# Twelve of the sixteen steps of each pass of a two-layer attention kernel written as a hardware loop instead of straight code

## The chip, the cores and the metric

The kernel runs on one core of one Trainium2 chip. The core has five engines that each run their own instruction stream: PE (TensorE, matrix products), DVE (VectorE), ACT (ScalarE), POOL (GpSimd) and SP (SyncE, which here issues all DMAs). They meet only through semaphores. The metric is the device time of one execution in microseconds (us), as the median of several.

## The reference

Two transformer layers over x of shape (16, 256, 256), 16 heads of 16, with a context of the same shape. Cut to what is computed:

```
layer 0:  t = ln(x);  x += attn(t, t, mask) @ Wo + bo;  x += ctx @ Wg + bg
          x += relu(ln(x) @ W1 + b1) @ W2 + b2
layer 1:  t = ln(x);  x += attn(t, t, causal) @ Wo
          t = ln(x);  x += attn(t, ctx, no mask) @ Wo
          x += relu(ln(x) @ w1 + b1) @ w2 + b2
attn:     p = softmax(q k^T / 4 + bias) per head;  p @ v
```

## The kernel before

The work is cut into three passes over the batch: pass 0 is layer 0, pass 1 is the causal self-attention of layer 1, pass 2 its cross-attention and the perceptron behind it. A pass has 16 tasks, one for each batch element of 256 tokens, so there are 48 tasks. Weights are kept as a high and a low part, and the dense products are three matmuls each (line 451, and line 713 for the second matrix of the perceptron).

The program is a software pipeline. A `Step` s looks at six tasks at once: `nxt2` (s+2, input loaded and normalised), `nxt` (s+1, its q, k, v made and sent through DRAM into `q_stack` and `k_stack`), `cur` (s, scores and softmax, head by head), `prev` (s-1, output projection), `old` (s-2, perceptron) and `older` (s-3, whose store must be through). Each step has 16 slots, one per head of `cur`. In every slot each engine does its share for that head (PE: scores at line 509, transposes or keyed scores at 523 and 557, products with v at 587) and a fixed piece of the other tasks' work. The order on each engine is that of the code: there is no scheduler. `s_ps` and `t_ps` have two buffers each, so PE cannot run more than two heads ahead of DVE (`u_done`) and ACT (`e_done`, `pt_even`, `pt_odd`).

Every wait names a semaphore and a value that it must have reached. `Event.after` and `DmaEvent.after` work that value out from the task: with a batch number known when the program is built it is a constant. Both also have a form for a task whose batch is `2 * i + c`, with `i` the counter of a loop; this form is a sum of a constant and a multiple of `i`.

In the kernel before, `steps` calls the body of each engine for s = -2 to 49, one after the other. So each engine's program is 52 steps of straight code, without a branch inside them. Three things depend on the number s: the loading of weight units (`UNIT_LOAD_AT`) and their splitting (`UNIT_AT`), and the first task of a pass. They lie in the steps -2 to 1, 14 to 18 and 30 to 33.

Of the kernel before, what the change touches and what calls it, by code (L numbers as in the profile page):

```python
# [32 lines left out]
B, S, D = 16, 256, 256  # L33
H, HD = 16, 16
# [6 lines left out]
NPASS = 3  # L41
# [3 lines left out]
NTASK = NPASS * B  # L45
# [58 lines left out]
        self.prev, self.old, self.older = at(-1), at(-2), at(-3)  # L104

def steps(body):

    for s in range(-2, NTASK + 2):
        body(Step(s))  # L110

class Event:
# [31 lines left out]
def two_layers(nc, x, ctx, mask, wa, wm1, wm2, cols, rows, ident, out):  # L145
    with ExitStack() as es:
# [179 lines left out]
        def _(sp):  # L326
# [11 lines left out]
            def slot(st, h):  # L338
                if st.s is not None and (st.s, h) in UNIT_LOAD_AT:
                    u = UNIT_LOAD_AT[st.s, h]  # L340
                    if u:
                        sp.wait_ge(unit_hi, u)
                        sp.wait_ge(unit_lo, u)
                    dram, place, _, _ = unit_io(u)
                    sp.dma_start(place, dram).then_inc(unit_landed, 16)
# [43 lines left out]
                if h == 7 and has(st.nxt):  # L389
# [8 lines left out]
                    for m in range(KC):  # L398
                        heads = slice(8 * m, 8 * m + 8)
                        if st.prev:  # L400
                            done = s_mm if has(st.prev, (0,)) else st_mm
                            sp.wait_ge(done.sem, done.after(st.prev, 8 * m + 8))
                            sp.sem_inc(passed, 1)
                        sp.wait_ge(q_written[m].of(t), q_written[m].after(t))
                        sp.sem_inc(passed, 1)
                        row = 0
                        for part, n in RUNS:
                            sp.dma_start(q_stack[row:row + n * HD, t.par, heads].rearrange("r h s -> r (h s)"),
                                         parts[t.par, 0, m, part].rearrange("d h s -> d (h s)").unsqueeze(1)
                                         .to_broadcast([HD, n, H // KC * S])).then_inc(stacked[m].of(t), 16)  # L410
                            row += n * HD
                        sp.wait_ge(k_written[m].of(t), k_written[m].after(t))
                        sp.sem_inc(passed, 1)
                        row = 0
                        for _, n in RUNS:
                            sp.dma_start(k_stack[row:row + n * HD, t.par, heads].rearrange("r h s -> r (h s)"),
                                         parts[t.par, 1, m, 0:n].rearrange("j d h s -> d j (h s)"))\
                                .then_inc(stacked[m].of(t), 16)
                            row += n * HD
# [9 lines left out]
                if h == 15 and has(st.old, MLP):  # L429
# [2 lines left out]
                    dst = x_mid[0, st.old.b] if st.old.p == 0 else out[st.old.b]  # L432
                    sp.dma_start(tokens(dst), y_sb[:, :, :]).then_inc(stored.of(st.old), 16)

            steps(lambda st: [slot(st, h) for h in range(H)])
            for b in (B - 2, B - 1):
                sp.wait_ge(stored.of(Task(NPASS - 1, b)), stored.after(Task(NPASS - 1, b)))
                sp.sem_inc(passed, 1)
# [3 lines left out]
        def _(pe):  # L442
# [162 lines left out]
            def slot(st, h):  # L605
# [124 lines left out]
                if t:  # L730
                    values(st, t, c)

            steps(lambda st: [slot(st, h) for h in range(H)])

        @block.scalar
        def _(act):
# [43 lines left out]
            def slot(st, h):  # L781
# [95 lines left out]
                if has(st.cur, (0,)):  # L877
                    probs(st, h)

            steps(lambda st: [slot(st, h) for h in range(H)])  # L880

        @block.vector
        def _(dve):
# [69 lines left out]
            def slot(st, h):  # L954
# [146 lines left out]
                if st.s is not None:  # L1101
                    for u in UNIT_AT.get((st.s, h), ()):
                        dve.wait_ge(unit_landed, 16 * (u + 1))
                        unit_users_done(dve, u)
                        _, place, hi, _ = unit_io(u)
                        v.tensor_copy(hi, place).then_inc(unit_hi, 1)

            dve.sem_inc(y_done.sem, 1)
            steps(lambda st: [slot(st, h) for h in range(H)])  # L1110

        @block.gpsimd
        def _(pool):
# [43 lines left out]
            def slot(st, h):  # L1158
# [51 lines left out]
                if st.s is not None:  # L1210
                    for u in UNIT_AT.get((st.s, h), ()):
                        pool.wait_ge(unit_hi, u + 1)
                        _, place, hi, lo = unit_io(u)
                        sub(lo, place, hi, unit_lo)

            steps(lambda st: [slot(st, h) for h in range(H)])

# [31 lines left out]
```

## Time and profile before

| | |
|---|---|
| median of 3 runs | 1629.67 us (1625.86 to 1632.24) |
| profiled execution | 1625.86 us, its span 1624.1 us |
| granted TensorE clock, mean of the span | 0.97 |
| PE busy | 1448.7 us (89%) |
| DVE, ACT, POOL busy | 1193.5, 1033.5, 835.1 us |
| DMA | 187.07 MB |

The profile is a hardware record of one execution. "PE" is the matmuls, "PEld" the loading of the stationary operand, which overlaps them. Waits, semaphore instructions, register instructions and branches are not counted as busy. Where an engine stood idle and nothing that the profile knows released it, the profile says "issue". The chain is the series of instructions and waits that ended last, followed back from the end.

### The profile page before, as it was taken

What the parts mean: (1) busy time and instruction counts of PE and PEld (TensorE: products, weight loads), DVE (VectorE), ACT (ScalarE), POOL (GpSimd) and SP (SyncE); (2) the same over time, 40 slices, a digit from 0 to 9 for tenths busy, and PEclk for the clock granted to TensorE, in tenths of its full rate; (3) what the DMA queues carried; (4) which work ended last, traced back from release to release, by engine and by line L of the source; (5) the groups of instructions that cost most, each with busy time, mean ns of one, the idle gap of its engine ahead of it and who ended that gap; (6) DMA issues with size and microseconds to landing.
All of it is one profiled execution on the core that took longest, in us unless ns stands there. A gap on an engine that the chain in (4) does not pass through costs nothing.

```text
span 1624.1 us, 39350 instructions
## 1 busy us (share of the span) xinstructions
PE 1448.7 (89%) x13568; PEld 1184.2 (73%) x13568; DVE 1193.5 (73%) x3871; ACT 1033.5 (64%) x2089; POOL 835.1 (51%) x1125
## 2 busy tenths in 40 slices
PE   2799999999999999878887888888999999999986
PEld 2578888888888888765665656656777777777766
DVE  3788878888888887767777677787677776777642
ACT  3677777777777775555666656666666566665652
POOL 4455544545555565544434444545565555656533
PEclk8899999999999999989999999999999999999999
DMA  4554433443344443444454454554344433344200
GB/s 134 163 147 120 120 105 105 116 121 105 112 117 124 125 124 92 131 124 135 113 144 124 112 146 120 158 145 117 97 111 119 117 100 103 105 119 123 79 20 13
DMA packets 163605, 187.07 MB, mean 115 GB/s; under 512 B 15953, under 2 KB 140241, under 8 KB 163409
## 3 DMA queue, kind: packets, MB, share of 16 engines
q1 hardware_dynamic: 163408, 184.57, 40.1%
q8 instruction: 110, 1.80, 0.5%
q14 instruction: 87, 0.70, 0.2%
HBM read 125.78 MB, written 58.72 MB: 114 GB/s over the span
## 4 chain that ended last, share of the span: by engine, by line
PE 59%; ACT 15%; DVE 14%; issue 8%; POOL 2%; DMA 1%; SPq 1%; DVEq 0%; ACTq 0%; POOLq 0%
PE d_ps L451 23%; PE d_ps L713 8%; PE o_ps L587 8%; PE s_ps L509 6%; PE t_ps L523 6%; DVE prob L915 4%; ACT prob_t L761 4%; PE t_ps L557 3%; ACT q_stack L769 3%; PE m_ps L458 3%; ACT xt_hi L776 1%; ACT h_f L853 1%; DVE top L900 1%; DVE stats L921 1%; DVE q_part L1017 1%
## 5 line engine op out<-in xcount | busy, mean ns | idle before, releaser
L761 ACT ACTIVATE prob_t<-t_ps 128x384 f32<-128x384 f32 (+1 forms) x512 | 275.7, 550 | 354.8 <-PE t_ps L557 189.3
L509 PE MATMUL s_ps<-k_stack,q_stack 96*128 96x256 bf16 (+1 forms) x1536 | 288.9, 270 | 81.0 <-DVE top L915 50.1
L752 ACT ACTIVATE prob<-prob,neg_max 128x256 f32<-128x256 f32 x512 | 233.5, 509 | 115.3 <-DVE neg_max L915 113.1
L509 PEld LDWEIGHTS s_ps<-k_stack,q_stack 96*128 96x128 bf16 x1536 | 116.1, 99 | 175.9 <-issue 68.2
L557 PE MATMUL t_ps<-q_stack,k_stack 108*128 108x256 bf16 (+1 forms) x1024 | 205.5, 267 | 29.8 <-ACT prob_t L761 27.4
L1137 POOL TENSOR_TENSOR h_lo<-h_f,h_hi 128x512 fp32r<-128x512 f32 x128 | 164.9, 1288 | 119.8 <-DVE h_hi L1032 119.8
L915 DVE CUSTOM_DVE_ANT_0 prob<-s_ps,bias_sb 128x256 f32<-128x256 f32 x512 | 193.3, 418 | 30.3 <-PE s_ps L509 29.8
L900 DVE TENSOR_REDUCE top<-s_ps 128x2 f32<-128x512 f32 x256 | 172.6, 682 | 46.8 <-PE s_ps L509 43.3
L915 DVE CUSTOM_DVE_ANT_0 prob<-s_ps,causal 128x128 f32<-128x128 f32 (+1 forms) x512 | 157.4, 352 | 54.5 <-PE s_ps L509 52.9
L587 PE MATMUL o_ps<-prob_t,v_sb 128*17 128x256 f32 (+1 forms) x3072 | 195.4, 373 | 0.0
L451 PE MATMUL d_ps<-x2t_hi,w_hi 128*128 128x256 f32 x512 | 156.6, 306 | 15.3 <-ACT k_f L834 10.3
L523 PE MATMUL t_ps<-ident_sb,prob 128*128 128x128 f32 x1024 | 156.8, 275 | 4.4 <-DVE prob_t L1095 4.3
L713 PE MATMUL d_ps<-w_hi,h_hi 128*128 128x256 f32 x512 | 147.5, 288 | 4.3 <-POOL h_lo L1137 4.3
L713 PE MATMUL d_ps<-w_lo,h_hi 128*128 128x256 f32 x512 | 147.7, 288 | 0.1
L713 PE MATMUL d_ps<-w_hi,h_lo 128*128 128x256 f32 x512 | 147.5, 288 | 0.0
L451 PE MATMUL d_ps<-x2t_lo,w_hi 128*128 128x256 f32 x512 | 145.1, 283 | 0.0
L451 PE MATMUL d_ps<-x2t_hi,w_lo 128*128 128x256 f32 x512 | 145.1, 283 | 0.0
L769 ACT ACTIVATE q_stack<-o_ps 12x1024 bf16<-12x1024 f32 x128 | 130.2, 1017 | 10.1 <-PE o_ps L536 6.3
L992 DVE STREAM_TRANSPOSE o_q<-o_ps 128x256 f32<-128x256 f32 x128 | 57.6, 450 | 101.6 <-PE o_ps L587 100.6
L523 PEld LDWEIGHTS t_ps<-ident_sb,prob 128*128 128x128 f32 x1024 | 119.7, 142 | 14.6 <-issue 9.6
L557 PEld LDWEIGHTS t_ps<-q_stack,k_stack 108*128 108x128 bf16 x1024 | 87.2, 100 | 58.9 <-ACT prob_t L761 36.7
L587 PEld LDWEIGHTS o_ps<-prob_t,v_sb 128*17 128x17 f32 x3072 | 71.8, 98 | 72.0 <-issue 27.5
(127 smaller groups left out, 4051.2 us busy)
## 6 DMA issues: line engine op xcount, KB each, us to landing
parts<-q_part SPq DMA_DIRECT2D x96, 192.0 KB, 2.3
parts<-k_part SPq DMA_DIRECT2D x96, 192.0 KB, 2.3
q_stack<-parts SPq DMA_DIRECT2D x96, 192.0 KB, 3.3
k_stack<-parts SPq DMA_DIRECT2D x96, 192.0 KB, 3.3
q_stack<-parts SPq DMA_DIRECT2D x96, 128.0 KB, 3.1
k_stack<-parts SPq DMA_DIRECT2D x96, 128.0 KB, 3.2
ct_kept<-ct_hl SPq DMA_DIRECT2D x16, 512.0 KB, 3.5
x_in<-x_mid SPq DMA_DIRECT2D x32, 256.0 KB, 3.0
```

What stands on the lines that cost most here:

```text
L451: last = mm(dst, lhs, rhs, start=(opens and n == 0), stop=(closes and n == len(terms) - 1))
L509: last = mm(s_ps[:, h % 2, q * S:q * S + n], q_stack[0:ROWS, t.par, head_of(t, h), q * P:(q + 1) * P], k_stack[0:ROWS, t.par, head_of(t, h ...
L523: last = nc.tensor.transpose(t_ps[:, h % 2, c:c + P], prob[:, h % 4, q, k * P:(k + 1) * P], ident_sb[:, :])
L557: last = mm(t_ps[:, h % 2, k * S:k * S + S - lo], k_stack[:, t.par, HEAD[h], k * P:(k + 1) * P], q_stack[:, t.par, HEAD[h], lo:S], start=T ...
L587: last = mm(o_ps[32 * j:32 * j + VW, lo:S], v_sb[:, t.par, k, head_of(t, h), :], prob_t[:, h % 8, k * S:k * S + S - lo], start=(k == 0), s ...
L713: last = mm(d_ps[:, 0, t * D:(t + 1) * D], lhs, rhs, start=(f == 0 and n == 0), stop=(f == FT - 1 and n == 2))
L752: last = nc.scalar.activation(prob[:, h % 4, q, :], prob[:, h % 4, q, :], ACT.Exp, bias=neg_max[:, h % 4, q:q + 1], scale=-1.0)
L761: nc.scalar.activation(prob_t[:, h % 8, 0:n], t_ps[:, h % 2, 0:n], ACT.Exp, scale=-1.0)\
L769: nc.scalar.activation(rows, o_ps[ROWS:ROWS + TOP, S:2 * S].unsqueeze(1).to_broadcast([TOP, CH, S]), ACT.Copy).then_inc(top_row.sem, 1)
L900: v.tensor_reduce(top[:, h // CH % 2, :, h % CH], s_ps[:, h % 2, :].rearrange("p (q k) -> p q k", q=TT), AX_X, ALU.min).then_inc(u_done.se ...
L915: last = v.tensor_tensor_reduce(prob[:, h % 4, q, 0:n], s_ps[:, h % 2, q * S:q * S + n], bias, 1.0, HUGE, ALU.add, ALU.min, least)
L1137: g.tensor_tensor(dst, a, b, ALU.subtract).then_inc(done, 1)
```

## The change

`steps` now takes the engine as well. It calls the body for s = -2 to 1 as before. Then, for each pass p, it opens a hardware loop on that engine (`Fori`) with six rounds; the body of a round holds two steps, j = 0 and 1, for tasks 2 + 2i and 3 + 2i of the pass. After the loop come four steps of straight code: the last two of this pass and the first two of the next one (or, behind pass 2, the two steps that drain the pipeline). The steps are the same 52, in the same order, with the same work in each slot. All five engines' programs get the three loops; each engine loops by itself, without a barrier.

```diff
-def steps(body):
-
-    for s in range(-2, NTASK + 2):
-        body(Step(s))
+def steps(eng, body):
+
+    for s in range(-2, 2):
+        body(Step(s))
+    for p in range(NPASS):
+        with eng.Fori(0, (B - 4) // 2) as i:
+            for j in range(2):
+                body(Step(p=p, j=j, i=i))
+        for s in range(B * p + B - 2, B * p + B + 2):
+            body(Step(s))
@@ each of the five engines, here PE
-            steps(lambda st: [slot(st, h) for h in range(H)])
+            steps(pe, lambda st: [slot(st, h) for h in range(H)])
```

Inside a loop a wait's value and a DMA's address hang on `i`, so the program has register instructions (REGISTER_ALU, or several packed in one, shown as ISA without operands) that work them out. The lines of the changed kernel are 6 higher than those before (509 is 515, 523 is 529, and so on).

First place: PE, where a step ends in pass 0 and the next begins (before). `s_ps` holds scores, `t_ps` the transposed probabilities, `o_ps` the products with v; what stands in brackets are the semaphores waited for.

```order
L509 MATMUL s_ps<-k_stack,q_stack 128x256 [waits u_done]
L509 MATMUL s_ps<-k_stack,q_stack 128x256
L523 MATMUL t_ps<-ident_sb,prob 128x128 [waits pt_even,p_done]
L523 MATMUL t_ps<-ident_sb,prob 128x128 x3
L509 MATMUL s_ps<-k_stack,q_stack 128x256 [waits u_done,stacked_half0_0]
L509 MATMUL s_ps<-k_stack,q_stack 128x256
L523 MATMUL t_ps<-ident_sb,prob 128x128 [waits pt_odd,p_done]
L523 MATMUL t_ps<-ident_sb,prob 128x128 x3
```

The same engine in the changed program: the end of a round of the loop of pass 0.

```order
L512 REGISTER_ALU
L515 MATMUL s_ps<-k_stack,q_stack 128x256 [waits u_done]
L515 MATMUL s_ps<-k_stack,q_stack 128x256
L525 REGISTER_ALU [waits p_done]
L529 MATMUL t_ps<-ident_sb,prob 128x128 [waits pt_even]
L529 MATMUL t_ps<-ident_sb,prob 128x128 x3
L112 REGISTER_ALU
L112 COMPARE_AND_BRANCH
```

And its beginning, to which that branch goes back five times.

```order
L112 ISA
L512 ISA [waits stacked_half0_0]
L515 MATMUL s_ps<-k_stack,q_stack 128x256 [waits u_done]
L515 MATMUL s_ps<-k_stack,q_stack 128x256
L520 REGISTER_ALU
L523 ISA [waits p_done]
L529 MATMUL t_ps<-ident_sb,prob 128x128 [waits pt_odd]
L529 MATMUL t_ps<-ident_sb,prob 128x128 x3
```

No matmul has moved. Between the last of one step and the first of the next stand a counter, a branch and two register instructions, and a register instruction stands ahead of most waits; some carry a wait themselves.

Second place: DVE at the same point of pass 0, before (the end of one step and the beginning of the next).

```order
L915 ISA prob,neg_max<-s_ps,bias_sb 128x256 [waits s_mm,t_mm]
L915 ISA neg_max 128x1
L915 ISA prob,neg_max<-s_ps,bias_sb 128x256
L915 ISA neg_max 128x1
L1100 CAST xt_hi<-tf_a 128x512 [waits v_mm,xt_f]
L915 ISA prob,neg_max<-s_ps,bias_sb 128x256 [waits bias_done,s_mm,t_mm]
L915 ISA neg_max 128x1
```

And after, the end of a round.

```order
L904 REGISTER_ALU
L921 ISA prob,neg_max<-s_ps,bias_sb 128x256 [waits s_mm,t_mm]
L921 ISA neg_max 128x1
L921 ISA prob,neg_max<-s_ps,bias_sb 128x256
L921 ISA neg_max 128x1
L1106 CAST xt_hi<-tf_a 128x512 [waits v_mm,xt_f]
L112 REGISTER_ALU
L112 COMPARE_AND_BRANCH
```

Here too nothing moved; the branch comes behind the last work of the step.

Third place: PE in pass 1, the rows of line 536 that turn the rounded score maxima (`top_part`), before.

```order
L509 MATMUL s_ps<-k_stack,q_stack 128x128 [waits u_done]
L509 MATMUL s_ps<-k_stack,q_stack 128x256
L536 MATMUL o_ps<-ident_bf,top_part 12x128 [waits o_done,top_3]
L536 MATMUL o_ps<-ident_bf,top_part 12x128
```

And after.

```order
L512 REGISTER_ALU
L515 MATMUL s_ps<-k_stack,q_stack 128x128 [waits u_done]
L515 MATMUL s_ps<-k_stack,q_stack 128x256
L535 REGISTER_ALU
L538 REGISTER_ALU [waits top_3]
L542 MATMUL o_ps<-ident_bf,top_part 12x128 [waits o_done]
L542 MATMUL o_ps<-ident_bf,top_part 12x128
```

The wait for `top_3` is now carried by a register instruction, ahead of the matmul. In all, a round of the loop has, on PE, 616 matmuls of the program with 120 other instructions in pass 0, 376 with 109 in pass 1, and 512 with 124 in pass 2; before, the others were 68, 38 and 44 for two steps, all of them bare waits.

## Rows read from the trace of the kernel before

**Rows 1.** The page: busy time, and the span in 40 slices.

```profile
PE 1448.7 (89%) x13568; PEld 1184.2 (73%) x13568; DVE 1193.5 (73%) x3871; ACT 1033.5 (64%) x2089; POOL 835.1 (51%) x1125
PE   2799999999999999878887888888999999999986
```

**Rows 2.** Busy time in two steps of pass 0, 1 and 2 (start:end, span).

```profile
206.10:280.10 74.00, 73.10 (x683) 64.94 (x682) 61.03 (x214) 53.49 (x125) 38.48 (x32) 1.00 0.39 115
280.10:354.10 74.00, 73.10 (x683) 64.93 (x682) 61.14 (x214) 53.47 (x125) 38.48 (x32) 1.00 0.41 115
818.30:868.80 50.50, 42.05 (x441) 31.34 (x441) 36.65 (x171) 30.79 (x56) 22.28 (x46) 0.93 0.43 121
1231.00:1299.00 68.00, 64.08 (x578) 50.77 (x577) 49.04 (x98) 43.73 (x80) 39.25 (x60) 1.00 0.40 110
```

**Rows 3.** The chain by line, in the same stretches of pass 0, 1, 2.

```profile
by line: PE d_ps L451 34.8%; PE t_ps L523 15.9%; PE d_ps L713 15.5%; PE s_ps L509 8.9%; PE o_ps L587 8.0%; PE m_ps L458 3.5%; DVE prob L915 3.5%; issue 3.1%; PE m_ps L601 2.4%; DVE prob_t L1095 1.7%; DVE xt_hi L1100 0.9%; DVE x_hat L935 0.8
...
by line: issue 13.6%; PE d_ps L451 12.1%; PE o_ps L587 10.7%; DVE prob L915 10.6%; PE t_ps L557 6.1%; PE s_ps L509 5.6%; DVE q_part L1017 4.5%; PE m_ps L458 4.1%; PE t_ps L561 3.7%; ACT xt_hi L776 3.5%; ACT tf_a L776 2.6%; DVE x_in L935 2.6
...
by line: PE d_ps L451 18.4%; ACT prob_t L761 10.5%; issue 9.5%; ACT q_stack L769 9.0%; PE o_ps L587 5.8%; PE d_ps L713 5.6%; PE t_ps L557 5.4%; ACT h_f L853 5.0%; DVE top L900 3.8%; PE s_ps L509 3.7%; ACT xt_hi L776 3.0%; ACT tf_b L776 3.0%
```

**Rows 4.** DMA queues of the span; queues 8 and 14 bring instructions.

```profile
q1 hardware_dynamic: 163408, 184.57, 40.1%
q8 instruction: 110, 1.80, 0.5%
q14 instruction: 87, 0.70, 0.2%
```

**Rows 5.** The same in 206.1 to 280.1 us, two steps of pass 0.

```profile
q8 instruction: 5, 0.08, 0.6%
q14 instruction: 4, 0.03, 0.1%
```

**Rows 6.** DMA issues: KB each, median us from issue to landing.

```profile
stage<-wm SPq DMA_DIRECT2D x4, 1024.0 KB, 5.3
ident_sb<-ident SPq DMA_DIRECT2D x1, 64.0 KB, 1.9
cols_sb<-cols SPq DMA_DIRECT2D x1, 20.0 KB, 1.8
```

**Rows 7.** Waits in 206.1 to 280.1 us (pass 0): us, times, longest.

```profile
PEld s_ps L509 <- issue: 2.5, 6, 0.4
...
PEld o_ps L587 <- issue: 1.0, 6, 0.2
PEld t_ps L523 <- issue: 1.0, 2, 0.5
```

**Rows 8.** Waits in 818.3 to 868.8 us (pass 1).

```profile
PEld s_ps L509 <- DVE top L915: 5.9, 7, 1.3
PEld s_ps L509 <- issue: 3.3, 6, 1.1
...
PEld o_ps L536 <- issue: 1.2, 6, 0.3
...
PEld o_ps L587 <- issue: 0.7, 3, 0.3
```

**Rows 9.** Waits in 1231.0 to 1299.0 us (pass 2).

```profile
PEld d_ps L451 <- issue: 2.1, 2, 1.1
...
PEld o_ps L536 <- issue: 1.7, 8, 0.2
PEld o_ps L587 <- issue: 1.7, 8, 0.2
```

**Rows 10.** Waits of PE's loads, whole span.

```profile
PEld s_ps L509 <- issue: 68.2, 137, 1.7
...
PEld o_ps L587 <- issue: 27.5, 136, 0.4
```

**Rows 11.** Waits of SP's queue, whole span.

```profile
SPq L431 <- DVE y_sb L1087: 402.0, 31, 29.8
SPq L383 <- DVE q_part L1017: 391.7, 48, 13.2
```

More of the change, by code:

```diff
@@ L433, in slot @@
                     sp.dma_start(tokens(dst), y_sb[:, :, :]).then_inc(stored.of(st.old), 16)
-            steps(lambda st: [slot(st, h) for h in range(H)])
+            steps(sp, lambda st: [slot(st, h) for h in range(H)])
             for b in (B - 2, B - 1):
@@ L731, in slot @@
                     values(st, t, c)
-            steps(lambda st: [slot(st, h) for h in range(H)])
+            steps(pe, lambda st: [slot(st, h) for h in range(H)])
         @block.scalar
@@ L878, in slot @@
                     probs(st, h)
-            steps(lambda st: [slot(st, h) for h in range(H)])
+            steps(act, lambda st: [slot(st, h) for h in range(H)])
         @block.vector
@@ L1109, in _ @@
             dve.sem_inc(y_done.sem, 1)
-            steps(lambda st: [slot(st, h) for h in range(H)])
+            steps(dve, lambda st: [slot(st, h) for h in range(H)])
         @block.gpsimd
@@ L1214, in slot @@
                         sub(lo, place, hi, unit_lo)
-            steps(lambda st: [slot(st, h) for h in range(H)])
+            steps(pool, lambda st: [slot(st, h) for h in range(H)])
 def kernel(**inputs):
```

## Prediction

> **What bounds the kernel now.** I read the page's busy times first, then the windows of two steps in each pass, then the chain in these windows, and last the waits. PE is the busiest engine with 89% of the span, and its slices are at 9 in the first and the last third and at 8 in the middle [rows 1]. Two steps of pass 0 take 74.0 us twice in a row, with PE busy for 73.1 [rows 2]: that pass is PE's work end to end, and its chain is nearly all PE lines [rows 3]. Two steps of pass 1 take 50.5 us with PE busy for 42.05; its chain goes round PE, DVE and ACT, and 13.6% of it is "issue", time in which an engine was waited for that itself waited for nothing recorded. Two steps of pass 2 take 68.0 us, PE 64.08, and the chain changes between PE and ACT, with 9.5% issue [rows 2, 3]. So in pass 0 whatever stops PE is paid in full, and in the other two what stops any of three engines is paid at least in part.
>
> Code reaches the engines as they go. Queue 8 brought 110 pieces of 1.80 MB / 110 = 16.4 KB, queue 14 brought 87 pieces of 0.70 MB / 87 = 8.0 KB [rows 4]. PE alone ran 2 x 13568 matmuls and loads [rows 1], 247 for each of the 110 pieces, and in the two steps of pass 0 five pieces came for 2 x 683 of them, 273 each [rows 2, 5]; so queue 8 is PE's and a piece holds some 250 of its instructions, and queue 14 serves the others with pieces of half that size. In straight code this costs nothing that I can see: PE is 99% busy in pass 0 while five pieces arrive.
>
> **The change part by part.**
>
> *The branch back.* Each loop has six rounds, so it jumps back five times; three loops make 15 jumps, 50 to 74 us apart [rows 2]. The round that it goes back over is long: on PE 2 x 683 = 1366 matmuls and loads in pass 0, 882 in pass 1 and 1156 in pass 2 [rows 2], or 5.5, 3.6 and 4.7 pieces of 250. DVE ran 214, 171 and 98 counted instructions in the same stretches, ACT 125, 56 and 80, POOL 32 to 60 [rows 2]; with their waits and register instructions DVE's round spans two to three pieces of some 125 and the others' mostly more than one piece boundary. The first piece of a round has long been passed when the round ends, and what was being fetched is the piece behind the loop. I take it that the piece at the loop's head must be fetched anew while the engine stands.
>
> What a fetch with the engine standing costs is not in the trace of before, which shows fetches ahead of need alone. From below it is nothing. From the rows: the smallest DMA, 20 KB, took 1.8 us from issue to landing [rows 6], most of it fixed, and a piece for PE spent 0.5% x 16 x 1624 / 110 = 1.2 us in its DMA engine, 1.4 in pass 0 (0.6% x 16 x 74 / 5) [rows 4, 5], because it goes through one engine behind data. I take 1.8 + 1.2 = 3.0 us. The far row is the 1 MB load with 5.3 us [rows 6], the upper end for a fetch.
>
> In pass 0 PE's 3.0 us are the price. DVE, ACT, POOL and SP make their own jumps at the same place of the program, within a head (74 / 32 = 2.3 us) of PE's, and have 13 us and more of room in two steps; their stop lies beside PE's. In pass 1 they don't have that cover: PE already waits for DVE there [rows 8], and a DVE that stands just after PE has come back holds the scores two heads on. I add 1.0 us, and 0.5 in pass 2, where PE is again near its full time. So 5 x (3.0 + 4.0 + 3.5) = 52.5 us.
>
> The Trainium skill, in "Runtime: NRT & Kernel Launch", section "Instruction fetch mechanics", says the same of the mechanism: code is prefetched in sequence only, the instruction memory is two blocks, and a taken branch out of that window stops the engine for a DMA. The trace agrees as far as the even arrival of pieces goes (110 for PE over the span); no row shows a taken branch.
>
> *The register instructions.* Before a wait in the loop its value is worked out. On PE a round has 120, 109 and 124 instructions beside the matmuls instead of 68, 38 and 44. Where PE waits for another engine anyway, the step before the wait is hidden. It is paid where PE's queue is empty and the profile shows "issue": in two steps 6 + 6 + 2 = 14 places in pass 0 [rows 7], 6 + 6 + 3 = 15 in pass 1 [rows 8], and 6 + 2 + 8 + 8 = 24 in pass 2 [rows 9] (its first 6, for `s_ps`, read as those of pass 0 do, 2.5 us [rows 7]), which last 4.5, 5.2 and 8.0 us together. An issue gap has a mean of 0.2 us in its short form (27.5 / 136) [rows 10], and behind a bare wait that is the cost of one blocking step with all that follows it. A plain register step more is a part of this; I take a quarter, 0.05 us, for each: 53 places x 0.05 x 6 rounds = 15.9 us. From below it is nothing; from above each gap would double, (4.5 + 5.2 + 8.0) x 6 = 106 us. I stay near the low end because most values can be computed while earlier work is queued. On DVE and ACT the same steps fall into engines that are 83 and 72% busy at most, behind queued work; I cost them at nothing there.
>
> *SP.* Its DMAs get an address from a register, and SP stops at its jumps too. SP waits 402 and 392 us for two lines alone, 8 to 13 us each time [rows 11]: the work is issued as early as its data allow, and the stacks that it fills are read a third of a step later. Nothing, while such gaps last.
>
> *Entry and exit.* The jump into a loop goes to the next instruction, and the last round falls through; nothing. *Less code.* The program is shorter, but a round that is read anew brings the same pieces; all instruction traffic is 0.7% of the DMA engines' time [rows 4], so nothing is gained.
>
> *Sum.* 1625.9 of the profiled execution + 52.5 + 15.9 = 1694.3 us. The median of the runs is 3.8 us above that execution, so the forecast is **1698 us**, 4.2% slower.
>
> **The rivals.**
>
> *The code stays at hand.* If an engine's memory keeps the pieces that it has passed and holds a round, a jump costs a short gap, 0.2 to 0.5 us by the issue gaps (27.5 / 136 and 68.2 / 137) [rows 10]; 15 x 0.35 = 5 us, with the 16 us of register steps 1625.9 + 21 = 1647, as a median about 1651 (1638 to 1666). For it: no row says how much is kept. Against it: five pieces come for every two steps of pass 0, and PE's round is longer than that. The Trainium skill's "Advanced Engine Details and Errata", section "ISA Cache", gives TensorE 128 KB, four times the others' memory; taken as room for passed code that would hold PE's round, and its "Control Flow Timing" prices a compare-and-branch at about 108 ns, 1.6 us for 15, an estimate. The same page speaks of only two lines, so the case is open for PE and less so for DVE.
>
> *The stops add up.* PE, DVE and ACT stand one after the other, each released by the one before: 3 x 3.0 us at each of 15 jumps, 135 us, with 16 us for registers 1777, as a median 1781. It decides if an engine meets its jump only after PE has resumed, which takes a lag of over 3 us; the two buffers of scores allow two heads, 4.6 us in pass 0 and 3.2 in pass 1. The same end is reached if every issue gap doubles (106 + 52.5 us).
>
> *Not slower.* The stops hide behind queued work. PE's queue would have to hold 3 us of matmuls at the end of a round, about 25 of them; but the last work there is four transposes behind a wait. Then the time is that of before, 1622 to 1638. It decides where the fetch for the head is begun before the jump. Against it is PE's 99% in pass 0: nothing there can be given back. A real gain needs fetches that disturb now, and I see none.
>
> **How the numbers follow.** The forecast has 0.60, with 1665 to 1725 as its own range (fetches of 2 to 4.5 us, register steps from nothing to 0.1 us). Code at hand 0.20, stops added or gaps doubled 0.10, not slower 0.10. Cutting a tenth off at each end gives 1642 to 1740. About 0.5% (8 us) is what a measurement can tell from no change. Of "not slower" 0.03 is faster and 0.07 the same; of "code at hand" 0.03 falls under 1638. So faster 0.03, same 0.10, slower 0.87.
>
> **What would show it.** In the windows of two steps, pass 0 grows from 74.0 to 77 us with a single idle stretch of PE of about 3 us after a transpose of line 529, and instruction pieces arrive in it; pass 1 grows by 4 to 5 us and pass 2 by 4 to 5. DVE has a gap of its own within a head of PE's. If the gap on PE is under 0.5 us the code is at hand; if two or three engines' gaps lie end to end, the stops add. Steps outside the loops (for instance around the change of passes) must be as before. If pass 0 grows with no gap at the round's end, the register steps are the cost and I was wrong in their size.

## The result and the profile after

The changed kernel takes 1637.32 us (median of 7 runs, 1634.95 to 1639.01); the kernel before, timed beside it, 1629.97 us (7 runs, 1625.86 to 1632.24). The ratio is 1.0051, with a 95% interval from 1.004 to 1.0062 (it rests on more runs than the two medians, whose own ratio is 1.0045): slower by half a per cent, where 4.2% were forecast. The profiled execution took 1637.11 us.

The page of the changed kernel: span, busy times, slices, DMA queues and the chain by engine.

```profile
span 1635.3 us, 43530 instructions
...
PE 1455.0 (89%) x13568; PEld 1185.1 (72%) x13568; DVE 1187.3 (73%) x3871; ACT 1031.3 (63%) x2089; POOL 836.3 (51%) x1125
...
PE   2799999999999999877888888888999999999986
...
q1 hardware_dynamic: 163408, 184.57, 40.4%
q8 instruction: 42, 0.69, 0.2%
q14 instruction: 61, 0.50, 0.1%
...
PE 61%; DVE 12%; issue 11%; ACT 10%; POOL 2%; DVEq 1%; DMA 1%; SPq 1%; ACTq 1%; POOLq 0%
```

The busy times are within 0.6% of [rows 1]; what has changed is the fetching of code. PE's queue 8 brought 42 pieces instead of 110, and queue 14, which serves the other engines, 61 instead of 87 [rows 4]. A loop that had to be read anew each round would have kept both numbers.

The windows of two steps, two pairs of pass 0, one of pass 1, one of pass 2; the columns are those of [rows 2].

```profile
173.50:249.00 75.50, 73.46 (x685) 64.90 (x686) 61.18 (x216) 53.35 (x125) 38.41 (x32) 1.00 0.39 112
249.00:324.40 75.40, 73.39 (x681) 64.85 (x681) 61.10 (x215) 53.29 (x125) 38.41 (x32) 1.00 0.40 112
752.50:803.20 50.70, 42.53 (x443) 31.31 (x442) 35.55 (x171) 30.78 (x57) 22.64 (x46) 0.93 0.46 125
1243.00:1311.00 68.00, 64.07 (x579) 50.80 (x578) 49.11 (x99) 43.62 (x81) 39.16 (x61) 1.00 0.38 108
```

Two steps of pass 0 take 75.4 to 75.5 us where they took 74.0 [rows 2]; pass 1 takes 50.7 instead of 50.5, and pass 2 has not changed by a tenth. By the first `x_in` transpose of each step, the steps of pass 0 last 37.1 and 38.3 us in turn, five times over; before, each lasted 37.0. So the loss sits at the five jumps of pass 0: 5 x 1.45 = 7.3 us, and that is the difference of the medians (7.35). The two profiled executions are further apart, 11.2 us in the span. The rest of that is two places behind the loss where the granted clock fell in this execution and not in that of before: it is 0.83 and 0.77 in the first two rows below, and 1.00 in before's at the same tasks. They make 1.5 and about 2 us. They aren't the jumps' doing: in `pe_alone` (see the experiments), where nothing stops, the clock is 0.83 at the first of these places too, in the third row.

```profile
1104.00:1114.00 10.00, 7.58 (x56) 4.61 (x54) 5.16 (x13) 7.15 (x14) 2.74 (x6) 0.83 0.33 101
1550.00:1565.00 15.00, 12.41 (x93) 8.09 (x86) 6.48 (x13) 8.48 (x15) 2.87 (x9) 0.77 0.12 36
...
1094.30:1104.30 10.00, 7.58 (x56) 4.47 (x54) 6.50 (x15) 6.59 (x11) 2.74 (x6) 0.83 0.42 129
```

Whose stop is it? The instruction queues in a round of pass 0 (173.5 to 249.0 us).

```profile
q1 hardware_dynamic: 7360, 8.39, 38.6%
q14 instruction: 5, 0.04, 0.2%
```

PE's queue 8, with five pieces in such a stretch before [rows 5], is gone, and five pieces of queue 14 are there. In the round that DVE enters at 248.5 us they come at 249.5, 251.9, 257.8, 286.7 and 314.2 us; the last three are 27.5 to 28.9 us apart, the time in which DVE gets through some 128 of the round's 345 instructions. DVE and then PE at the jump of 248.5 us; what stands in brackets is idle time and what ended it.

```profile
250.18 0.42 DVE L1106 CAST xt_hi<-tf_a 128x512 fp32r<-128x512 f32 x1
251.73 0.42 DVE L921 CUSTOM_DVE_ANT_0 prob<-s_ps,bias_sb 128x256 f32<-128x256 f32 x1 [1.13 <-PE t_ps L529]
```

```profile
250.32 0.39 PE L515 MATMUL s_ps<-k_stack,q_stack 96*128 96x256 bf16 x2 [0.28 <-DVE neg_max L921]
...
252.56 0.39 PE L515 MATMUL s_ps<-k_stack,q_stack 96*128 96x256 bf16 x2 [0.98 <-DVE neg_max L921]
...
253.26 0.63 PE L529 MATMUL t_ps<-ident_sb,prob 128*128 128x128 f32 x4 [0.30 <-DVE prob_t L1101]
```

The views don't list branches, but the trace has them. An engine's instruction stream runs ahead of its work: DVE's branch is issued at 248.5 us, while 2 us of work are still queued, and its stream goes on at 251.3, 2.82 us later. The queued work ends at 250.6, and DVE is idle for 1.13 us. PE had gone round its own jump at 246.1 us without an idle moment, and comes to a stand one and two heads later for want of DVE's scores: 0.28 + 0.98 + 0.30 us. The name in DVE's bracket misleads: PE's transposes ended at 251.15 us, before DVE's stream went on.

From one branch to the next instruction of the same stream, over all 15 jumps of each engine:

| engine | instructions in a round, pass 0 / 1 / 2 | pass 0, us | pass 1 and 2, us |
|---|---|---|---|
| PE | 1481 / 989 / 1276 | 0.27 to 0.30 | 0.27 to 0.29 |
| DVE | 345 / 272 / 186 | **2.82 to 2.95** | 0.29 to 0.35 |
| ACT | 207 / 128 / 167 | 0.24 to 0.26 | 0.24 to 0.26 |
| POOL | 52 / 79 / 101 | 0.24 to 0.27 | 0.16 to 0.27 |
| SP | 112 / 98 / 111 | 0.28 to 0.32 | 0.29 to 0.30 |

### The profile page after: what moved, and what is told of

It reads as the page before. It is cut to its first block, busy times and chain, and to the rows that moved or that the text cites. A ratio compares the mean times of both kernels' runs of the same rounds, so it can differ in the third digit from the quotient of the medians.

```text
span 1635.3 us, 43530 instructions
## 1 busy us (share of the span) xinstructions
PE 1455.0 (89%) x13568; PEld 1185.1 (72%) x13568; DVE 1187.3 (73%) x3871; ACT 1031.3 (63%) x2089; POOL 836.3 (51%) x1125
## 4 chain that ended last, share of the span: by engine, by line
PE 61%; DVE 12%; issue 11%; ACT 10%; POOL 2%; DVEq 1%; DMA 1%; SPq 1%; ACTq 1%; POOLq 0%
PE d_ps L457 24%; PE d_ps L719 9%; PE o_ps L593 8%; PE s_ps L515 6%; PE t_ps L529 6%; PE t_ps L563 4%; PE m_ps L464 3%; DVE prob L921 3%; ACT prob_t L767 2%; ACT q_stack L775 1%; POOL k_f L1143 1%; DVE top L906 1%; ACT xt_hi L782 1%; ACT h_f L859 1%; PE t_ps L567 1%
## 5 line engine op out<-in xcount | busy, mean ns | idle before, releaser
L593 PEld LDWEIGHTS o_ps<-prob_t,v_sb 128*17 128x17 f32 x3072 | 71.8, 98 | 71.8 <-issue 27.3
```

The source lines that it names most:

```text
L593: last = mm(o_ps[32 * j:32 * j + VW, lo:S], v_sb[:, t.par, k, head_of(t, h), :], prob_t[:, h % 8, k * S:k * S + S - lo], start=(k == 0), s ...
```

## The experiments

Two questions: does DVE's stop in pass 0 make the whole loss, and what decides whether a jump stops an engine? The theory: an engine keeps a few pieces of code, four of 128 instructions on DVE and eight of some 250 on PE, one of them the piece fetched ahead. A round that lies in three (seven) of them is still there at the jump. DVE's round of pass 0 has 345 instructions and would fit into three if it began near a piece's start; it begins at slot 89 of a piece (a slot is an instruction's place in its piece, 0 to 127; `dve_shift50` showed the 89, its expectation still reckoned with 97), and 89 + 345 = 434 makes four.

**One loop written out, one loop alone.** The five engines have three loops each, fifteen in all. In `dve0_straight` DVE runs pass 0 as straight code; the other 14 stay. `dve0_alone` is the reverse: DVE's pass 0 is the only loop. `pe_alone` has PE's three loops and no other.

```diff
+        if p in looped:
             with eng.Fori(0, (B - 4) // 2) as i:
                 for j in range(2):
                     body(Step(p=p, j=j, i=i))
+        else:
+            for s in range(B * p + 2, B * p + B - 2):
+                body(Step(s))
```

> The changed kernel, with DVE's pass 0 alone put back to straight code; the other 14 loops stay. Theory: the whole loss is DVE standing 2.8 us after each of its five jumps in pass 0, of which 1.5 us reach the time, because that round (345 instructions of DVE) is the only one that its instruction memory does not hold. Then this runs like the kernel before: ratio 0.999 to 1.002, two steps of pass 0 back at 74.0 us. Rival one, the register steps on all engines cost: then 4 of 5 engines still pay and the ratio stays at 1.003 to 1.005. Rival two, each jump of PE costs about 0.3 to 0.5 us: the same 1.003 to 1.005.

> The kernel before, with DVE's pass 0 alone written as a loop; the other 14 stay straight. Theory: all of the loss comes back, 5 x 1.5 = 7.5 us, ratio 1.004 to 1.006, two steps of pass 0 at 75.5 us. Rivals (register steps or jumps of all engines): a fifteenth to a fifth of the loss, ratio 1.000 to 1.001.

> The kernel before, with PE alone looped, in rounds of two steps (1481, 989 and 1276 instructions, at most seven pieces of 256); the other four engines stay straight. It measures what the register steps and the jumps cost where no code is missed. Theory: 0.3 us for each jump behind queued matmuls, and register steps of 0.03 us that run ahead of their waits: two steps of pass 0 at 74.0 to 74.2 us, ratio 1.000 to 1.001. Rival, the prediction's own term: 53 places x 0.05 us x 6 rounds = 16 us, ratio 1.008 to 1.011.

Measured: `dve0_straight` 1.0011 [0.9998, 1.0024], 1630.48 us; `dve0_alone` 1.0044 [1.0031, 1.0057], 1636.35 us; `pe_alone` 1.0009 [0.9998, 1.0019], 1630.80 us. 74 us of pass 0 in each of the three, in that order.

```profile
175.00:249.00 74.00, 73.03 (x684) 64.89 (x680) 61.02 (x215) 53.31 (x124) 38.44 (x32) 1.00 0.40 114
```

```profile
175.00:249.00 74.00, 72.17 (x664) 64.32 (x662) 59.61 (x210) 52.97 (x124) 38.38 (x32) 1.00 0.40 115
```

```profile
175.00:249.00 74.00, 73.05 (x681) 64.94 (x680) 61.03 (x216) 53.31 (x125) 38.43 (x32) 1.00 0.39 114
```

The first and the third get through two steps in 74.0 us, 681 and 684 matmuls, as before; the second only through 664, since its two steps take 75.4 (stops of 2.79 to 2.92 us at the five jumps). One loop out of fifteen carries nearly the whole loss, and the fourteen others with all their register instructions cost 0.1%, which isn't told apart from nothing. The rival of `pe_alone`, my own term of register steps, is refuted.

**The same loop at another place of its piece.** `dve_shift50` puts 50 bare semaphore increments ahead of DVE's first loop, `dve_shift56_start` 56 of them at the very start of DVE's program, where it waits for its first data anyway. Nothing else changes.

```diff
     for s in range(-2, 2):
         body(Step(s))
+    if ahead:
+        ahead()
...
-            steps(dve, lambda st: [slot(st, h) for h in range(H)])
+            steps(dve, lambda st: [slot(st, h) for h in range(H)], lambda: [dve.sem_inc(passed, 1) for _ in range(50)])
```

```diff
+            for _ in range(56):
+                dve.sem_inc(passed, 1)
```

> The changed kernel, with 50 semaphore increments ahead of DVE's first loop and nothing else. They move the round of 345 from slot 97 to slot 19 of its 128-instruction piece, so it lies in 3 pieces instead of 4. Theory: the memory holds four pieces, one of them fetched ahead; a round in 3 pieces stays, the gap of 2.8 us after the jumps is gone and with it 7.5 us: ratio to before 0.999 to 1.002, and no instruction fetch of queue 14 in the loops of pass 0. Rival: it is the length (345 over some limit) and not the place; then nothing changes, 1.004 to 1.006. If register steps cost, nothing changes either.

> The changed kernel, with 56 semaphore increments at the very start of DVE's program, where DVE stands 5 us for the constants; an increment took 0.093 us in the run before, so they are hidden. By the crossing seen there the round of pass 0 moves to slot 17 and that of pass 1 to slot 4 of their pieces: both lie in 3 pieces. Theory (four pieces kept, one of them fetched ahead): no jump misses in any pass, all 15 take 0.3 us, two steps of pass 0 take 74.2 us, ratio to before 0.999 to 1.002. Rival, the length counts and not the place, and the gain in pass 0 of the run before had another cause: pass 0 stays at 75.5 us and the ratio at 1.004 to 1.006.

Measured: `dve_shift50` 1.0222 [1.0204, 1.0239], 1667.69 us, far outside what was expected. Yet in pass 0, for which it was made, all was as expected: jumps of 0.30 to 0.35 us, no instruction piece between 180 and 480 us, two steps in 74.2 us.

```profile
180.00:254.20 74.20, 73.24 (x684) 64.90 (x680) 61.06 (x215) 53.38 (x125) 38.48 (x32) 1.00 0.40 113
754.00:811.00 57.00, 44.85 (x442) 33.05 (x440) 35.34 (x171) 30.67 (x57) 22.68 (x46) 0.88 0.41 111
```

The loss went elsewhere. The step with the increments was longer by 6.4 us, once; 5.0 of them are the increments' own (50 x 0.093 us and the gap of a piece boundary behind the 40th, from which I could tell the slots). The rest is pass 1, where two steps now take 55.5 to 57 us instead of 50.5: its loop was shifted as well, from slot 76 to slot 126, and 126 + 272 = 398 makes four pieces. DVE and PE at the first jump there:

```profile
754.66 0.08 DVE L923 DVE_READ_ACCUMULATOR2_ANT top<- 128x1 f32 x1
760.45 0.29 DVE L923 CUSTOM_DVE_ANT_0 prob<-s_ps,causal 128x128 f32<-128x128 f32 x1 [5.71 <-issue]
```

```profile
761.15 0.50 PE L517 MATMUL s_ps<-k_stack,q_stack 96*128 96x128 bf16 x2 [4.11 <-DVE top L923]
```

DVE stands for 5.7 us, twice the stop of pass 0, since the head's piece holds only two instructions of the loop and the next one has to be fetched behind it. Five such jumps at some 6 us make 30 of the 36 us; a lower clock, 0.88 in the row above against 0.93 in [rows 2], has a part in them. I had looked at one loop of a program in which every later loop moves along.

`dve_shift56_start` was placed by that lesson: all three of DVE's loops lie in three pieces (slots 17, 4 and 92). It measured 1.0012 [1.0002, 1.0023], 1632.55 us, as expected: the fastest kernel with all fifteen loops, and still not faster than before.

```profile
173.50:247.70 74.20, 73.23 (x682) 64.93 (x681) 61.02 (x215) 53.32 (x125) 38.40 (x32) 1.00 0.41 113
748.00:797.00 49.00, 40.93 (x443) 30.62 (x442) 35.41 (x170) 30.76 (x57) 22.62 (x46) 0.97 0.46 128
1237.00:1305.00 68.00, 64.06 (x578) 50.78 (x577) 49.10 (x100) 43.60 (x81) 39.16 (x60) 1.00 0.38 108
```

```profile
249.13 0.42 DVE L1108 CAST xt_hi<-tf_a 128x512 fp32r<-128x512 f32 x1
249.46 0.42 DVE L923 CUSTOM_DVE_ANT_0 prob<-s_ps,bias_sb 128x256 f32<-128x256 f32 x1
```

The same two DVE instructions that stood 1.13 us apart in the changed kernel now follow each other with no gap. The work is equal and the number of instructions in the loop too; only the slot differs.

```diff
-        with eng.Fori(0, (B - 4) // 2) as i:
+        loop = (eng.bass.Fori(0, (B - 4) // 2, engines=[eng.engine], hint_back_edge=True)
+                if p == 0 and eng.engine == mybir.EngineType.DVE else eng.Fori(0, (B - 4) // 2))
+        with loop as i:
```

```profile
175.00:249.00 74.00, 73.04 (x680) 64.76 (x679) 60.84 (x215) 53.16 (x125) 38.47 (x32) 1.00 0.39 113
```

This loop still begins at slot 89 and lies in four pieces, yet in its rounds not one instruction piece was fetched, neither the head's nor another. So four pieces do have room. In the changed kernel a round brings five, and the fifth comes at 314.2 us, before the branch of 323.9: by its place it is the one behind the branch, and I read it as what pushes the head out. That reading fits all runs here; what the hint does inside isn't in the trace.

**Rounds too long for every engine.** `rounds_of_four` puts four steps into a round: 3 rounds, 2 jumps a loop. PE's round then has some 1970 instructions and more, over seven pieces in each pass. `pe_fours` does it with PE alone looped, `dve_fours` with DVE alone.

```diff
-        self.b = c if i is None else i * 2 + c
+        self.b = c if i is None else i * 4 + c
...
-        with eng.Fori(0, (B - 4) // 2) as i:
-            for j in range(2):
+        with eng.Fori(0, (B - 4) // 4) as i:
+            for j in range(4):
...
```

> The changed kernel with four steps a round and three rounds a loop: two jumps back in each loop instead of five, and rounds twice as long (PE 2953, 1970 and 2538 instructions, DVE 674, 537 and 365, ACT 401, 253 and 324). Theory: PE's memory holds eight pieces of 256, so PE now misses in all three passes; each miss stops it 3 to 4 us, pass 0 and 2 pay nearly all of it, pass 1 more: 6 jumps x 3.5 us = 21 us, ratio 1.010 to 1.015. Rival, PE keeps any round: only DVE misses, 2 x 1.5 us in pass 0 and about as much in pass 1, ratio 1.002 to 1.005. Rival, jumps cost as such: fewer jumps, ratio 1.002.

> The kernel before, with PE alone looped, in rounds of four steps (2953, 1970 and 2538 instructions, more than eight pieces of 256): two jumps in each pass, six in all, and every other engine in straight code. Theory: each jump stops PE for 3.4 to 3.9 us as in the run with all engines in fours; pass 0 and 2 pay it nearly whole, pass 1 part of it: 4 x 3.5 + 2 x 2.5 = 19 us, ratio 1.011 to 1.013. Rival: PE's queue of loaded matmuls and the others' lead hide half, 1.005 to 1.007; then the 6 to 7 us of pass 0 in that run came from several engines standing at once.

> The kernel before, with DVE alone looped, in rounds of four steps (674, 537 and 365 instructions; by their places in 6, 5 and 4 pieces, so all miss). Two jumps in each pass. Theory: the same stop of 2.8 us costs 1.5 us each in pass 0 as measured, 6 us each in pass 1 as with the shift of 50, and in pass 2 something between, 1 to 3 us: 3 + 12 + 4 = 19 us, ratio 1.008 to 1.014. Rival: a stop costs the same in every pass, 6 x 1.5 = 9 us, 1.0055.

Measured: `rounds_of_four` 1.0156 [1.0141, 1.0171], 1653.83 us, a little above what was expected; `pe_fours` 1.0127 [1.0113, 1.0142], 1649.32 us, as expected; `dve_fours` 1.0065 [1.005, 1.0079], 1640.01 us, less than expected. In the first, PE stops for 3.4 to 4.0 us at all six jumps, DVE for 2.8 to 3.0 at all six, and ACT, whose round has 401 instructions in pass 0, for 2.9 to 3.3 in that pass and not in the others (253 and 324). Queue 8 brings 127 pieces, more than straight code. PE in `rounds_of_four`, pass 0, and in `pe_fours`, pass 2:

```profile
248.49 0.39 PE L515 MATMUL s_ps<-k_stack,q_stack 96*128 96x256 bf16 x2 [1.87 <-issue]
```

```profile
1252.90 0.61 PE L519 MATMUL s_ps<-k_stack,q_stack 96*128 96x256 bf16 x2 [2.70 <-issue]
```

Here is the stop that the prediction had in mind, on PE and named "issue". In `pe_fours` the step with the jump is longer by 3.6 and 6.3 us in pass 0 and by 4.1 and 1.7 in pass 2. In pass 1, where a step takes 24.4 to 26.2 us before the change too, only the twelve looped steps together can be compared: 302.6 us against 299.9. The passes' own excess is 10.0, 2.7 and 5.7 us, 3.1 for each of the six jumps.

Why did the second jump of pass 0 cost 6.3 us, with a stop of 3.6 as at the first (3.9)? The granted clock accounts for part of it. Behind both stops TensorE's clock fell from 2.4 to 1.2 GHz for a while, and behind the second for longer; the rows' clock is the mean of these levels. Two rows at the first jump, two at the second:

```profile
242.70:252.00 9.30, 7.08 (x55) 4.94 (x54) 6.89 (x24) 4.46 (x10) 1.98 (x2) 0.82 0.27 79
252.00:262.00 10.00, 10.00 (x96) 8.63 (x91) 6.68 (x25) 7.57 (x19) 4.36 (x4) 1.00 0.11 37
394.30:404.00 9.70, 6.17 (x55) 4.56 (x53) 6.89 (x24) 4.41 (x10) 1.97 (x2) 0.90 0.28 83
404.00:414.00 10.00, 10.00 (x70) 8.87 (x65) 5.22 (x21) 6.98 (x17) 2.57 (x2) 0.75 0.09 30
```

Undisturbed steps of pass 0 have a clock of 1.00 [rows 2], and so it is in the changed kernel's pass 0, where PE idles for 0.3 to 1 us at a time. With DVE's and ACT's stops in addition, the two jumps of pass 0 cost 7.1 and 6.1 us in `rounds_of_four`; and yet the total (1.0156) is under what PE's and DVE's loops cost apart (1.27% + 0.65% = 1.92%): in part the stops lie beside each other.

In `dve_fours` I had expected 6 us for each jump of pass 1, taken from `dve_shift50`. The steps with these jumps are 1 to 2.6 us longer than those beside them, and the twelve steps of pass 1 together 3.6 us longer than before, 1.8 for each jump; in pass 0 a jump costs 1.2 to 1.3, in pass 2 0.3 to 0.4. The rival, one price of about 1.5 us for all, was nearer: the 6 us belonged to the double stop, not to pass 1. DVE at a jump in pass 0 and in pass 1:

```profile
251.62 0.42 DVE L925 CUSTOM_DVE_ANT_0 prob<-s_ps,bias_sb 128x256 f32<-128x256 f32 x1 [1.14 <-PE t_ps L533]
...
804.68 0.29 DVE L925 CUSTOM_DVE_ANT_0 prob<-s_ps,causal 128x128 f32<-128x128 f32 x1 [2.70 <-PE s_ps L519]
```

## Why the prediction was wrong

**The bound.** Right. Pass 0 is PE's work end to end, and what delays PE there is paid: DVE's 1.13 us of idle time came out as 1.4 to 1.5 us in the windows.

**"The piece at the loop's head must be fetched anew while the engine stands."** This is the step that failed. It was taken for every engine and every jump. It holds for DVE in pass 0 alone, 5 jumps of 75, and for PE, on which the sum rested, at none: 0.27 to 0.30 us, with no piece on queue 8 between 180 and 550, 760 and 1000, or 1180 and 1500 us. Of 52.5 us, 7.3 were there. I argued from the pace at which pieces arrive in straight code [rows 4, 5], and that shows how much is read, not how much is kept; no row of before shows how much is kept, and I should have let the rival weigh more than 0.20. From the runs: up to 1481 instructions of PE are kept and some 1970 aren't, and on DVE three pieces of 128 are kept, four are not (but for the run with the hint).

**The rule that I leant on.** The runs fit room for four pieces of 8.0 KB on DVE, and show a limit between 1481 and some 1970 instructions on PE, with pieces of 16.4 KB for about 250. The Trainium skill's "Runtime: NRT & Kernel Launch", section "Instruction fetch mechanics", is confirmed in that code is read in sequence and a jump out of the window stops for a DMA. Its window of two blocks is not: PE's rounds of 989 to 1481 instructions, four to six pieces of some 250, would have missed, and took 0.27 to 0.30 us. "Advanced Engine Details and Errata", section "ISA Cache", has the sizes that fit, 128 KB for TensorE and a quarter of it for the others (eight pieces of 16.4 KB, four of 8.0 KB). I had its figure in a rival and let its "two lines" count against it; the measurement decides for the size.

**The price of a stop.** Near in size: 3.0 us forecast, 2.8 to 2.95 on DVE and 3.4 to 4.0 on PE where they do stop. In part that is luck. The traces show the head's piece 1.0 to 1.5 us after the branch. It spends 0.3 to 0.7 us in its DMA engine on DVE and 0.9 to 1.4 on PE, where I took 1.2; the rest of the stop is 2.2 to 3.1 us and not the 1.8 of the smallest load, and on DVE the smaller piece made up for it.

**"Their stop lies beside PE's."** Wrong for the kernel as it is: PE has no stop beside which DVE's could lie, so DVE's came through with about half of its 2.85 us: 1.45 us against straight code, of which 0.2 stay when the stop is gone (two steps then take 74.2). The other half is covered by work queued ahead of the branch. The sign was in my own text, "In pass 1 they don't have that cover", and I didn't work it out for a PE that doesn't stop.

**The added 1.0 and 0.5 us in pass 1 and 2.** No stop, so nothing. Where DVE was made to stop there (`dve_fours`), it was 1.8 and 0.3 to 0.4 us: sizes of that order.

**The register instructions.** 15.9 us forecast. `pe_alone`, with all of PE's, is at 1.0009 and takes 74.0 us in pass 0; with all engines looped and no stop, two steps take 74.2, which is 0.2 x 6 = 1.2 us for the pass; with DVE's pass 0 straight it is 74.0, so they belong to DVE's loop, whose steps I had put at nothing. A record of one lasts 0.03 to 0.05 us on PE, near the 0.05 estimated; but PE's stream is ahead of its work, and even where the profile says "issue" the gaps did not grow: those ahead of `s_ps` came to 46.8 us (68.2 before), those ahead of `o_ps` to 27.3 (27.5) [rows 10].

```profile
PEld s_ps L515 <- issue: 46.8, 106, 1.4
...
PEld o_ps L593 <- issue: 27.3, 134, 0.4
```

**The rivals.** "The code stays at hand" named the mechanism that came true for 70 of 75 jumps, and its test (a gap under 0.5 us on PE) decided it. Its time, 1651, was off for the register term in it; its 5 us of short gaps are mostly hidden too. The time of before with DVE's five stops, 1629.97 + 7.3 = 1637.3, is the measured one. "The stops add up" didn't happen. "Not slower" gave 1622 to 1638 us, and 1637.32 lies in it, but not by its mechanism: PE had no stop to hide, half of DVE's wasn't hidden, and the kernel is slower, clear of noise. SP, entry and exit, and less code gave nothing that shows (`dve0_straight`, 1.0011), as forecast.

## What to carry to other kernels

Before a long hardware loop is priced, count each engine's instructions in a round, register and wait instructions included, and compare them with what that engine keeps; here the limit was three pieces of 128 on DVE and lay between 1481 and some 1970 instructions on PE, and a round within it jumped back in 0.3 us. If an engine is over it or just at it, the slot at which the head falls decides, and everything put ahead of it moves all later loops too; watch the instruction queues of the profile inside the loop: pieces that come again in each round mean that the loop is read again. The stop of an engine that isn't the bound is to be costed against the work queued on it, and not against a stop of the bound that may not take place.

## What the runs showed of the hardware

- A taken jump back to kept code is 0.16 to 0.35 us from branch to next instruction; a missed one 2.8 to 3.0 us on DVE, 2.9 to 3.3 on ACT, 3.4 to 4.0 on PE.
- A head in the last two slots of its piece made DVE stand for 5.7 us at a jump, two fetches in a row (`dve_shift50`).
- Equal code at slot 89 or 17 of a piece: 1.0051 or 1.0012 of the time before.
- Fifty semaphore increments in a row took 0.093 us each on DVE.
- Behind a stop of PE of 3.6 to 3.9 us in pass 0 the granted clock was 0.75 to 0.82 over some 10 us (`pe_fours`), and the jump cost up to 6.3 us.
- Why the granted clock dips in the changed kernel's profile at 1108 and 1555 us and not in before's stays open; it dips near the first of these in `pe_alone` too, which has no stop.
